# Query logits and key transposes in twos on two pairs of banks, and the inverse norms' product in the next step

## The chip, the cores and the metric

One core of a Trainium2 chip runs the whole program. The metric is device time in microseconds, the median over runs; smaller is better. PE is TensorE, DVE VectorE, ACT ScalarE, POOL GpSimd, SP the queue that issues most DMAs. Every engine takes its own instructions in order and waits at semaphores for the others.

## The reference

Cross attention with a channel softmax, then a gated feed-forward block on 4-bit weights, each added to a residual stream. Cut to what the kernel's stages compute:

```python
# x, ctx: (32, 64, 512).  Attention, 8 heads of 64:
q = Wq @ layernorm(x);  k = Wk @ ctx;  v = Wv @ ctx
q = softmax(q, over the head's 64 rows) * 64 ** -0.5
k = softmax(k, over the 512 columns)
context = einsum('bhdn,bhen->bhde', k, v)
out = einsum('bhde,bhdn->bhen', context, q)
out = Wo @ out + bo
out = out / max(norm(out, over rows), 1e-12) * g * 8
x = x + tanh(g_xattn) * out
# Feed-forward, inner width 1376, weights dequantised from 4 bits:
h = layernorm(x)
x = x + tanh(g_ffn) * ((silu(h @ Wg) * (h @ Wu)) @ Wd)
```

## The kernel before

The 32 batches go in 16 pairs of two times 64 rows, which fill 128 partitions. Attention runs as a software pipeline, one step for each pair `p` from 0 to 15, and a step `PAIRS` that drains it; the steps from 4 on are loops on the engines. The feed-forward block follows from about 402 us on. The change touches attention's steps from `p` = 2 on, called `residual` in the code; there are 14 of them.

In such a step PE works for three pairs at once. For pair `p` it computes query logits twice: transposed and rough in `t_logits` (for the maxima that DVE takes in `q_maxima`), and exact in `q_logits` with `less_max`, which subtracts the maxima. It computes key logits in `k_logits`, which DVE reduces in `k_maxima` and ACT exponentiates in `k_exps`, and transposes the exponentials in `k_transposed`. For pair `p - 1` it computes the query softmax's `denominators`, spreads their reciprocals over rows in `spread_reciprocals` (DVE multiplies with them in `normalise`), and builds `context` and `fold_context`. For pair `p - 2` it computes `output` and `squared_norms`, and `spread_inverse_norm` spreads the inverse norms over rows; DVE's `normed_and_gated` scales the output with them, and POOL adds it to the residual in `residual_added`.

The order of every engine's work is written out by hand, at the end of its `step` (PE L1293 to L1330, DVE L1685 to L1732, ACT L765 to L789, POOL L483 to L494). Four tiles t = 0 to 3 of 128 rows make up a pair's logits. PSUM's eight banks are four pairs: `dve_pair` for `t_logits` and the spread reciprocals; `k_pair` and `act_pair`, listed as `k_pairs`, on which `k_logits(t)` alternate; and `small_pair` for all sums of other kinds. In the part of a step after `q_max_rows`, `k_pair` holds the query logits of one tile after another (ACT's `q_exp_tile` reads them) and `act_pair` the key transposes of one tile after another (ACT's `k_transposed` reads them), so that PE waits on each for ACT's reading of the tile before.

The layernorm of the next pair runs in the same step: DVE's `layernorm_stats(p + 1)`, POOL's eight small instructions in `moments`, DVE's `layernorm_apply(p + 1)`, then ACT's `x_high(p + 1)`, which stands in ACT's order between the exponentials of key tiles 0 and 1. `k_logits(2)` and `k_logits(3)` wait until the exponentials of tiles 0 and 1 have been read out of their banks. The reciprocals of the denominators go through DMAs: ACT copies the sums out, SP reshapes them by four DMAs, DVE takes reciprocals, and SP gathers them by four more before `spread_reciprocals(0)`.

## Time and profile before

| what | us |
|---|---|
| median of 3 runs | 665.08 (663.89 to 665.49) |
| the profiled execution | 663.38 |
| its span, from the first to the last instruction | 661.5 |
| PE busy | 643.0 (97%) |
| DVE busy | 581.2 (88%) |
| ACT busy | 480.3 (73%) |
| POOL busy | 266.3 (40%) |

Busy shares are means over the whole span; what a wait costs has to be read from the stage in which it stands. PE's instructions overlap in the rows, since a matmul's modelled end lies after the next one's start: PE's own time is therefore read from start to start, and the difference between a row's start and the start of the next is what the row cost. The same holds, to a smaller degree, for DVE and ACT, whose next instruction may begin some 0.08 us ahead of the last one's end.

### The profile page before, as it was taken

Reading aid. Unit: us, or ns where it says so; the run is one execution under the profiler, and the core shown is the slowest. Engines: PE = TensorE matmul, PEld = TensorE weight load, DVE = VectorE, ACT = ScalarE, POOL = GpSimd, SP = SyncE. Lnnn points to the kernel's source line nnn. Section 1 sums busy time; section 2 is a strip of 40 time slices with the busy share of each in tenths; the row PEclk is TensorE's granted clock in tenths of the full one; section 3 lists DMA queues with packets and bytes.
Section 4 is the critical chain, followed back from the end, with each engine's and each line's share of the span. In section 5 each row is a group of like instructions: output and inputs, shape, how many; then the busy total and the mean of one; then the engine's idle time right before and its main releaser. Section 6 shows DMA issues by size and latency. Waiting matters only on the chain.

```text
span 661.5 us, 14311 instructions
## 1 busy us (share of the span) xinstructions
PE 643.0 (97%) x5097; PEld 330.9 (50%) x5097; DVE 581.2 (88%) x803; ACT 480.3 (73%) x846; POOL 266.3 (40%) x366
## 2 busy tenths in 40 slices
PE   7899999999999999999999998999999999999996
PEld 6454554555455456455445543445444544454443
DVE  7778898899899899889888849899999999988996
ACT  4886677677678667666767656778877887777775
POOL 6312323323332332332336265455444444444442
PEclk8999999999999999999999999999999999999999
DMA  4112422421340321222020000000000001000002
GB/s 120 37 34 76 100 53 56 103 78 27 102 95 15 94 82 40 50 82 78 12 86 21 6 10 2 1 1 0 1 33 32 1 1 44 22 0 17 37 12 63
DMA packets 30618, 28.57 MB, mean 43 GB/s; under 512 B 18623, under 2 KB 20810, under 8 KB 30578
## 3 DMA queue, kind: packets, MB, share of 16 engines
q1 hardware_dynamic: 28170, 27.37, 15.1%
q10 hardware_dynamic: 2408, 0.70, 0.5%
q8 instruction: 21, 0.34, 0.2%
q14 instruction: 19, 0.16, 0.1%
HBM read 22.06 MB, written 4.23 MB: 40 GB/s over the span
## 4 chain that ended last, share of the span: by engine, by line
PE 88%; ACT 4%; DVE 4%; issue 1%; POOL 1%; SPq 0%; DMA 0%; DVEq 0%; POOLq 0%
PE small_pair L1069 8%; PE pair L1358 8%; PE small_pair L1035 8%; PE pair L1359 7%; PE pair L1148 7%; PE pair L1021 6%; PE pair L1372 6%; PE pair L1381 6%; PE small_pair L1053 5%; PE pair L1178 4%; PE small_pair L1358 4%; PE pair L1133 4%; PE small_pair L1359 4%; ACT eq L682 3%; PE pair L1000 3%; PE pair L1158 2%
## 5 line engine op out<-in xcount | busy, mean ns | idle before, releaser
L1756 DVE SCALAR_TENSOR_TENSOR acc<-pair,scale_T,acc 128x512 f32<-128x512 f32 (+1 forms) x176 | 126.7, 747 | 12.1 <-PE pair L1359 5.9
L843 ACT ACTIVATE pair<-pair,rescale 128x512 f32<-128x512 f32 x119 | 74.9, 656 | 39.5 <-PE pair L1381 39.5
L1372 PE MATMUL pair<-in_hi,d_int 128*128 128x512 f32 (+1 forms) x176 | 100.7, 575 | 0.4 <-ACT in_hi L832 0.4
L1381 PE MATMUL pair<-in_lo,d_int 128*128 128x512 f32 (+1 forms) x176 | 100.2, 573 | 0.0
L673 ACT ACTIVATE ek<-pair,kneg 128x512 f32<-128x512 f32 x128 | 86.4, 682 | 17.9 <-DVE kneg L1617 17.9
L1358 PE MATMUL pair<-ek,w_gu 128*128 128x512 f16 (+1 forms) x235 | 91.1, 388 | 1.0 <-DVE acc L1756 0.7
L580 POOL TENSOR_TENSOR inter<-act_gate,acc 128x512 f32<-128x512 f32 (+1 forms) x43 | 55.0, 1278 | 86.7 <-ACT act_gate L825 86.7
L1359 PE MATMUL pair<-ekT,w_gu 128*128 128x512 f16 (+1 forms) x235 | 89.1, 379 | 0.0
L1622 DVE TENSOR_TENSOR eq<-eq,pair 128x1024 f32<-128x1024 f32 x64 | 77.7, 1213 | 11.0 <-PE pair L1133 11.0
L1612 DVE TENSOR_REDUCE qmax<-pair 128x16 f32<-128x1024 f32 x64 | 78.1, 1221 | 8.2 <-PE pair L1000 7.3
L682 ACT ACTIVATE eq<-pair 128x1024 f32<-128x1024 f32 x64 | 65.7, 1027 | 20.7 <-PE pair L1158 20.6
L1617 DVE TENSOR_REDUCE kneg<-pair 128x2 f32<-128x1024 f32 x64 | 77.8, 1216 | 0.5 <-PE pair L1021 0.3
L1756 DVE SCALAR_TENSOR_TENSOR acc<-small_pair,scale_T,acc 128x512 f32<-128x512 f32 (+1 forms) x88 | 65.8, 747 | 7.7 <-PE small_pair L1359 4.0
L589 POOL TENSOR_TENSOR in_lo<-inter,in_hi 128x512 fp32r<-128x512 f32 (+1 forms) x43 | 55.0, 1279 | 43.1 <-ACT in_hi L832 43.1
L678 ACT ACTIVATE ekT<-pair 128x1024 f32<-128x1024 f32 x64 | 65.4, 1022 | 5.3 <-PE pair L1178 5.3
L1069 PE MATMUL small_pair<-ekT,ctxT 128*64 128x512 f32 x256 | 64.6, 605 | 0.0
L461 POOL TENSOR_TENSOR rn_sq<-ss_max,minus_half 128x8 f32<-128x8 f32 x16 | 26.4, 1650 | 86.2 <-DVE ss_max L1546 86.2
L1035 PE MATMUL small_pair<-eq,fold 128*64 128x512 f32 x240 | 57.1, 598 | 0.0
L1178 PEld LDWEIGHTS pair<-ident,ek 64*128 64x128 f32 x1024 | 41.3, 138 | 21.5 <-issue 19.3
L1358 PEld LDWEIGHTS pair<-ek,w_gu 128*128 128x128 bf16 (+1 forms) x235 | 23.1, 98 | 54.7 <-issue 33.9
L1178 PE MATMUL pair<-ident,ek 64*128 64x64 f32 x1024 | 47.0, 226 | 0.8 <-ACT ek L673 0.7
L1358 PE MATMUL small_pair<-ek,w_gu 128*128 128x512 f16 (+1 forms) x117 | 45.4, 388 | 0.7 <-DVE acc L1756 0.7
(200 smaller groups left out, 1268.1 us busy)
## 6 DMA issues: line engine op xcount, KB each, us to landing
xall<-in_x SPq DMA_DIRECT2D x16, 256.0 KB, 2.6
ctx_raw<-in_ctx SPq DMA_DIRECT2D x16, 256.0 KB, 2.9
out_x<-xall SPq DMA_DIRECT2D x16, 256.0 KB, 2.0
zero<-zeros_plus SPq DMA_DIRECT2D x8, 344.0 KB, 5.9
packed<-in_L_ffn_gate_qweight SPq DMA_DIRECT2D x4, 688.0 KB
packed<-in_L_ffn_up_qweight SPq DMA_DIRECT2D x4, 688.0 KB
packed<-in_L_ffn_down_qweight SPq DMA_DIRECT2D x10, 256.0 KB
zero<-zeros_plus SPq DMA_DIRECT2D x5, 256.0 KB, 4.8
```

The lines of the kernel that those rows point to most:

```text
L673: act.activation(ek[:, b, t, :], k_pairs[t % 2][:, b, :], ACT.Exp, bias=kneg[:, b, t:t + 1], scale=-1.0, accum_out=ksum[:, k_slot(b, t):k_ ...
L682: act.activation(eq[:, par, t, :, :], k_pair[:, :, :], ACT.Exp).then_inc(q_exp, 1)
L1035: last = pe.matmul(small[1][half(b), :], fold[:, k_slot(b, t), :], eq[:, par, t, b, :], start=(t == 0), stop=(t == OT - 1))
L1069: last = pe.matmul(small[0][half(b), :].rearrange("c (t e d) -> c t e d", t=OT, e=2), ctxT[:, t, half(b)], heads, start=(t == 0), stop=(t ...
L1178: last = pe.transpose(act_pair[:, e, slot * DH:(slot + 1) * DH], ek[half(e), b, ot, t * P:(t + 1) * P], ident[half(e), half(e)])
L1358: pe.matmul(gu_bank[count % 3][0:w, :], lhsT, xT_hi[:, g, rows], start=True, stop=False)
L1359: pe.matmul(gu_bank[count % 3][0:w, :], lhsT, xT_lo[:, g, rows], start=False, stop=True).then_inc(gu_mm, 1)
L1372: pe.matmul(z_bank[nt], d_int[0:w, it, nt * P:(nt + 1) * P], in_hi[0:w, n % 2, :], start=it == 0, stop=False, skip_group_check=True)
L1381: pe.matmul(z_bank[nt], d_int[0:w, it, nt * P:(nt + 1) * P], in_lo[0:w, n % 2, :], start=False, stop=True, skip_group_check=True).then_inc ...
L1612: dve.tensor_reduce(qmax[:, t, :, 0:HEADS], dve_pair[:, :, :].rearrange("n b (h d) -> n b h d", d=DH), AX.X, ALU.max).then_inc(t_max, 1)
L1617: dve.tensor_reduce(kneg[:, :, t], k_pairs[t % 2][:, :, :], AX.X, ALU.min).then_inc(k_max, 1)
L1756: dve.scalar_tensor_tensor(out=acc[0:w, n % 2, m, :], in0=gu_bank[(8 * n + job) % 3][0:w, :], scalar=scale_T[0:w, it, 4 * m + g:4 * m + g ...
```

## The change

Three things change, all in steps from `p` = 2 on.

First, the banks and the order of the second part of a step. Query logits and key transposes of tile t both go to `k_pairs[t % 2]`. PE takes two tiles of query logits, then the two key transposes of the same tiles, then the next two of each; ACT reads them in the same order. A key transpose waits for ACT's exponentials of its own tile (same banks), query logits of tiles 2 and 3 wait for ACT's copies of the transposes of tiles 0 and 1, and the next step's `k_logits(0)` waits for the copy of transpose 2 in place of the last exponentials. `ctx_transposed` comes ahead of the transposes of tiles 2 and 3.

Second, `spread_inverse_norm` leaves the end of the step and stands in the next step between `k_logits(0)` and `denominators`, on bank `small[1]`; DVE's `normed_and_gated` follows to the next step, behind `k_maxima(0)`. `output(0)` then waits for it, and `denominators` no longer does.

Third, on DVE, `layernorm_stats` goes from ahead of `q_maxima(1)` to behind it, and `context_rows` from ahead of `normalise(3)` to behind it.

```diff
@@ -264,9 +264,7 @@
 
         def rn_bank(r2):
 
-            if not isinstance(r2, int):
-                return small[0][:, :]
-            return z_bank[0] if r2 == PAIRS - 2 else small[1 if r2 == PAIRS - 1 else 0][:, :]
+            return z_bank[0] if isinstance(r2, int) and r2 == PAIRS - 2 else small[1][:, :]
 
         def xT_bank(k):
 
@@ -275,6 +273,12 @@
         def y_rows():
 
             return small[1][:, :].bitcast(F16)[:, 0:N]
+
+        def q_pair(t, turns):
+            return k_pairs[t % 2 if turns else 0]
+
+        def kt_pair(t, turns):
+            return k_pairs[t % 2 if turns else 1]
 
         def y_columns(nt):
 
@@ -675,11 +679,11 @@
 
                 def k_transposed(t, back=0):
                     act.wait_ge(kt_mm, 4 * (p - back) + t + 1)
-                    act.activation(ekT[:, t, :, :], act_pair[:, :, :], ACT.Copy).then_inc(kt_evac, 1)
+                    act.activation(ekT[:, t, :, :], kt_pair(t, residual)[:, :, :], ACT.Copy).then_inc(kt_evac, 1)
 
                 def q_exp_tile(t):
                     act.wait_ge(q_mm, 4 * p + t + 1)
-                    act.activation(eq[:, par, t, :, :], k_pair[:, :, :], ACT.Exp).then_inc(q_exp, 1)
+                    act.activation(eq[:, par, t, :, :], q_pair(t, residual)[:, :, :], ACT.Exp).then_inc(q_exp, 1)
 
                 def denominators():
                     act.wait_ge(d_mm, r + 1)
@@ -784,6 +788,13 @@
                     context()
                     q_maxima()
                     k_exps(3)
+                if residual:
+                    for first_tile in (0, 2):
+                        q_exp_tile(first_tile)
+                        q_exp_tile(first_tile + 1)
+                        k_transposed(first_tile)
+                        k_transposed(first_tile + 1)
+                    return
                 for t in range(NT):
                     q_exp_tile(t)
                     k_transposed(t)
@@ -933,7 +944,9 @@
 
             def ffn_input(k):
 
-                if k == 3:
+                if k == 0:
+                    pe.wait_ge(kt_evac, 4 * PAIRS - 1)
+                elif k == 3:
                     pe.wait_ge(sT_ready, 4)
                 elif k == 2 * TPC:
                     pe.wait_ge(ss_evac, PAIRS)
@@ -1006,9 +1019,11 @@
                         return
                     if t == 0:
                         pe.wait_ge(c_lo, p + 1)
-                        if combine:
+                        if residual:
+                            pe.wait_ge(kt_evac, 4 * p - 1)
+                        if combine and isinstance(p, int) and p <= 2:
                             pe.wait_ge(q_exp, 4 * p)
-                        else:
+                        elif not combine:
                             pe.wait_ge(wT_lo_ready, 2)
                     elif t == 1:
                         if combine:
@@ -1041,10 +1056,7 @@
                     if not combine:
                         return
                     pe.wait_ge(q_exp, 4 * r + 4)
-                    if at_least(p, 3):
-                        pe.wait_ge(yn_ready, r - 1)
-                    else:
-                        pe.wait_ge(ct_evac, r + 1)
+                    pe.wait_ge(ct_evac, r + 1)
                     if isinstance(p, int) and p == 1:
                         pe.wait_ge(pool_consts, POOL_CONSTS)
                     for tt in range(2):
@@ -1140,12 +1152,16 @@
                     if t == 0:
                         pe.wait_ge(k_exp, 7 * p + 6)
                         pe.wait_ge(x_lo, p + 1)
+                    elif not residual:
+                        pe.wait_ge(q_exp, 4 * p + t)
+                    elif t == 1:
+                        pe.wait_ge(k_done, p + 1)
                     else:
-                        pe.wait_ge(q_exp, 4 * p + t)
+                        pe.wait_ge(kt_evac, 4 * p + t - 1)
                     cols = slice(t * P, (t + 1) * P)
                     for n, (w, v) in enumerate(((wqT_hi, xs_hi), (wqT_lo, xs_hi), (wqT_hi, xs_lo))):
                         for b in range(2):
-                            pe.matmul(k_pair[:, b, :], w[half(b), cols], v[half(b), par, :], start=(n == 0), stop=False)
+                            pe.matmul(q_pair(t, residual)[:, b, :], w[half(b), cols], v[half(b), par, :], start=(n == 0), stop=False)
 
                 def less_max(t):
                     if not project:
@@ -1155,7 +1171,7 @@
                         if not combine:
                             pe.wait_ge(wT_ready, 2)
                     for b in range(2):
-                        last = pe.matmul(k_pair[:, b, :], minus_spread[half(b), t, :], qmax_rows[half(b), :],
+                        last = pe.matmul(q_pair(t, residual)[:, b, :], minus_spread[half(b), t, :], qmax_rows[half(b), :],
                                          start=False, stop=True)
                     last.then_inc(q_mm, 1)
 
@@ -1163,7 +1179,9 @@
                     if not project:
                         return
                     pe.wait_ge(pool_consts, 2)
-                    if t > 0:
+                    if residual:
+                        pe.wait_ge(q_exp, 4 * p + t + 1)
+                    elif t > 0:
                         pe.wait_ge(kt_evac, 4 * (p - back) + t)
                     else:
                         pe.wait_ge(k_done, p + 1)
@@ -1175,7 +1193,7 @@
                             if residual:
                                 pe.wait_ge(ss_evac, r)
                         for e in range(2):
-                            last = pe.transpose(act_pair[:, e, slot * DH:(slot + 1) * DH],
+                            last = pe.transpose(kt_pair(t, residual)[:, e, slot * DH:(slot + 1) * DH],
                                                 ek[half(e), b, ot, t * P:(t + 1) * P], ident[half(e), half(e)])
                     last.then_inc(kt_mm, 1)
 
@@ -1195,15 +1213,16 @@
                     last.then_inc(ct_mm, 1)
 
                 def spread_inverse_norm():
-                    if not residual:
+                    if not at_least(p, 3):
                         return
-                    if isinstance(p, int) and p == 2:
+                    if isinstance(p, int) and p == 3:
                         pe.wait_ge(wT_ready, 3)
-                    pe.wait_ge(rn_gathered, 32 * r)
-                    pe.wait_ge(ct_evac, p + 1)
-                    pe.matmul(small[0][:, :], spread_batch[0:C, :], rn_rows[0:C, :], start=True, stop=True).then_inc(rn_mm, 1)
+                    pe.wait_ge(rn_gathered, 32 * (r - 1))
+                    pe.wait_ge(ct_evac, r + 1)
+                    pe.matmul(small[1][:, :], spread_batch[0:C, :], rn_rows[0:C, :], start=True, stop=True).then_inc(rn_mm, 1)
 
                 if drain:
+                    spread_inverse_norm()
                     denominators()
                     ffn_input(0)
                     ffn_input(1)
@@ -1292,6 +1311,7 @@
                     return
                 t_logits(0)
                 k_logits(0)
+                spread_inverse_norm()
                 denominators()
                 t_logits(1)
                 k_logits(1)
@@ -1312,21 +1332,20 @@
                 spread_reciprocals(0)
                 less_max(0)
                 context(3)
+                q_logits(1)
+                less_max(1)
                 k_transposed(0)
                 spread_reciprocals(1)
-                q_logits(1)
-                less_max(1)
                 k_transposed(1)
                 fold_context()
+                q_logits(2)
                 spread_reciprocals(2)
-                q_logits(2)
                 less_max(2)
-                k_transposed(2)
-                ctx_transposed()
-                spread_reciprocals(3)
                 q_logits(3)
                 less_max(3)
-                spread_inverse_norm()
+                spread_reciprocals(3)
+                ctx_transposed()
+                k_transposed(2)
                 k_transposed(3)
 
             step(0, 0, 0, True, False, False)
@@ -1685,9 +1704,11 @@
                 if project:
                     q_maxima(0)
                     k_maxima(0)
+                    if at_least(p, 3):
+                        normed_and_gated(p - 3)
+                    q_maxima(1)
                     if not last:
                         layernorm_stats(p + 1, i + par, 1 - par)
-                    q_maxima(1)
                     k_maxima(1)
                     if not last:
                         layernorm_apply(p + 1)
@@ -1699,6 +1720,7 @@
                     q_maxima(3)
                     k_maxima(3)
                 if drain:
+                    normed_and_gated(p - 3)
                     reciprocals()
                     second_stats(p - 3)
                     normalise(0)
@@ -1726,10 +1748,9 @@
                     less_zero(p, *weights, 1)
                 folded()
                 normalise(2)
+                normalise(3)
                 context_rows()
-                normalise(3)
                 key_sums()
-                normed_and_gated(r2)
 
             step(0, 0, 0, True, False, False)
             step(1, 0, 1, True, True, False)
```

## Rows read from the trace of the kernel before

**Rows 1.** The page, part 1: busy time, share of the span, instructions of each engine.

```profile
PE 643.0 (97%) x5097; PEld 330.9 (50%) x5097; DVE 581.2 (88%) x803; ACT 480.3 (73%) x846; POOL 266.3 (40%) x366
```

**Rows 2.** The windows view, one step: length, busy time of engines, granted clock, DMA.

```profile
181.40:205.20 23.80, 23.67 (x245) 12.41 (x242) 21.79 (x28) 17.11 (x31) 7.77 (x14) 1.00 0.30 71
```

**Rows 3.** The timeline of PE in one step: start, duration, line, operation, count.

```profile
184.35 0.71 PE L1178 MATMUL pair<-ident,ek 64*128 64x64 f32 x16
184.87 0.47 PE L1133 MATMUL pair<-rden_rows,spread 64*128 64x512 f32 x2
...
185.87 0.41 PE L1158 MATMUL pair<-qmax_rows,minus_spread 64*128 64x512 f32 x2
186.28 0.71 PE L1178 MATMUL pair<-ident,ek 64*128 64x64 f32 x16
...
187.55 0.50 PE L1133 MATMUL pair<-rden_rows,spread 64*128 64x512 f32 x2
...
188.80 0.66 PE L1178 MATMUL pair<-ident,ek 64*128 64x64 f32 x16
...
189.71 0.50 PE L1133 MATMUL pair<-rden_rows,spread 64*128 64x512 f32 x2
...
191.11 0.39 PE L1204 MATMUL small_pair<-rn_rows,spread_batch 64*128 64x512 f32 x1
...
191.80 0.50 PE L1000 MATMUL pair<-wqT_hi,xs_hi 64*128 64x512 f32 x2
192.40 0.50 PE L1021 MATMUL pair<-cs_hi,wkT_hi 64*128 64x512 f32 x2
...
193.29 1.92 PE L1053 MATMUL small_pair<-eq,head_sum 128*32 128x512 f32 x16
195.15 0.50 PE L1000 MATMUL pair<-wqT_hi,xs_hi 64*128 64x512 f32 x2
...
201.77 0.40 PE L1021 MATMUL pair<-cs_hi,wkT_hi 64*128 64x512 f32 x2
...
205.20 0.46 PE L1094 MATMUL pair<-ident,qmax 64*128 64x64 f32 x8
```

**Rows 4.** The timeline of PE, seven steps later.

```profile
359.60 1.92 PE L1053 MATMUL small_pair<-eq,head_sum 128*32 128x512 f32 x16
```

**Rows 5.** The timeline of DVE; in brackets the idle time before and what ended it.

```profile
188.45 1.21 DVE L1622 TENSOR_TENSOR eq<-eq,pair 128x1024 f32<-128x1024 f32 x1
...
191.60 0.70 DVE L1553 SCALAR_TENSOR_TENSOR yn<-small_pair,gate_col,y 128x512 f32<-128x512 f32 x1
192.34 1.23 DVE L1612 TENSOR_REDUCE qmax<-pair 128x16 f32<-128x1024 f32 x1
...
194.61 0.68 DVE L1455 BATCH_NORM_STATS2 stats<-xall 128x6 f32 x1
195.69 1.22 DVE L1612 TENSOR_REDUCE qmax<-pair 128x16 f32<-128x1024 f32 x1 [0.40 <-PE pair L1000]
...
200.10 0.55 DVE L1626 RECIPROCAL rden<-den_sq 128x64 f32<-128x64 f32 x1 [1.00 <-DMA den_sq<-den]
...
201.26 1.23 DVE L1612 TENSOR_REDUCE qmax<-pair 128x16 f32<-128x1024 f32 x1
```

**Rows 6.** The timeline of ACT in the same step.

```profile
186.32 1.03 ACT L682 ACTIVATE eq<-pair 128x1024 f32<-128x1024 f32 x1 [0.19 <-PE pair L1158]
...
191.32 1.02 ACT L682 ACTIVATE eq<-pair 128x1024 f32<-128x1024 f32 x1 [0.37 <-PE pair L1158]
...
198.53 0.63 ACT L642 ACTIVATE xs_hi<-xn 128x512 fp32r<-128x512 f32 x1 [1.31 <-DVE xn L1461]
...
200.30 0.20 ACT L673 ACTIVATION_READ_ACCUMULATOR ek<-pair,kneg 128x1 f32 x1
```

**Rows 7.** The timeline of POOL: the first and the last of layernorm's eight instructions.

```profile
195.37 0.19 POOL L86 TENSOR_TENSOR ln_work<-stats 128x2 f32<-128x2 f32 x1 [1.57 <-DVE stats L1455]
...
197.26 0.55 POOL L86 TENSOR_TENSOR ln_work<-ln_work,minus_half 128x1 f32<-128x1 f32 x1
```

## Prediction

> **What bounds the kernel now.** I read the page's busy shares first: PE 97%, DVE 88%, ACT 73% [rows 1]. Then the windows view of one step of attention, to see whether that holds where the change is: in 23.8 us PE is busy 23.67, DVE 21.79, ACT 17.11, and the granted clock is 1.00, the level of 2.4 GHz [rows 2]. So PE comes first, but DVE has only 2 us to spare. Then the timelines, from start to start. The product `denominators` starts at 193.29 and, seven steps later, at 359.60 [rows 3, 4]: 166.31 / 7 = 23.76 us a step, and what is said of one step holds for all of them, 14 with the edits.
>
> I count from PE's `t_logits(0)` at 191.80. `k_logits(0)` starts at +0.60, `denominators` +1.49, `t_logits(1)` +3.35, `k_logits(3)` +9.97, `q_max_rows` +13.40; from `q_max_rows` to the next `t_logits(0)` is 23.76 - 13.40 = 10.36 [rows 3]. The reader is to see two things. PE's waits are short: `k_logits(0)` starts 0.06 after ACT's last query exponential (191.32 + 1.02), some 0.3 late [rows 3, 6]; the key transposes of tile 1 start at 186.28, 0.2 after `less_max(1)` from 185.87 would have let them [rows 3]. Together with smaller ones, at `spread_reciprocals` and `t_logits(3)`, I make it about 1.2 us a step. And between +2.8 and +8.7 a chain runs over three engines: DVE's `layernorm_stats` (194.61, 0.68 long), POOL's eight instructions (195.37 to 197.81), DVE's `layernorm_apply`, ACT's `x_high` (198.53), then the exponentials of key tile 1, whose last record ends at 200.50 [rows 5, 6, 7]. `k_logits(3)`, which needs their banks, starts at 201.77 [rows 3]: 1.27 us of slack. DVE waits 1.00 us for the denominators' DMA before its reciprocals at 200.10 [rows 5].
>
> **The change part by part.**
>
> *First half of a step, to `q_max_rows`.* `k_logits(0)` now waits for ACT's copy of transpose 2 (below), and starts at about +0.78 in place of +0.60. The norm's product comes behind it. At the end of the step it costs 0.2 now (the transposes beside it take 191.11 to 191.80, 0.69; those of tile 0 took 184.35 to 184.87, 0.52) [rows 3]; in front of `denominators` I give it 0.23, one pair of products: five pairs took 187.55 to 188.80, 1.25, and four 184.87 to 185.87, 1.00 [rows 3], so about 0.23 a pair and 0.1 ahead of the first, where the shape of the tiles changes. So `denominators` starts at 0.78 + 0.89 + 0.23 = +1.9 (0.89 is 192.40 to 193.29), and `t_logits(1)` 1.86 later (193.29 to 195.15), at +3.75, 0.4 late [rows 3].
>
> On DVE `normed_and_gated` (191.60 to 192.34, 0.74) goes from ahead of `q_maxima(0)` to behind `k_maxima(0)` [rows 5]. The end of a step gains nothing by it: `t_logits(0)` doesn't ask for it. It ends at +3.6, ahead of `output(0)` at about +4.9, which now waits for it with all later PE work behind; that wait costs nothing. POOL's addition behind it fits before layernorm's instructions.
>
> But `q_maxima(1)` can't start before `t_logits(1)` + 0.54 (195.69 - 195.15), +4.29 [rows 3, 5], and `layernorm_stats` now stands behind it: it starts at 4.29 + 1.14 = +5.43 in place of +2.81. (1.14 is 192.34 on to the next start in the same engine, 1.23 long less the 0.08 by which instructions overlap.) The chain follows: stats end +6.11; POOL's instructions take 197.81 - 195.29 = 2.52 from that end [rows 5, 7], +8.63; `layernorm_apply` then ends at about +9.2 and `x_high` starts at +9.25 in place of +6.73. From `x_high` to the end of tile 1's exponentials is 200.50 - 198.53 = 1.97 [rows 6], so +11.22, and `k_logits(3)` starts at +11.27. PE would be there at 9.97 + 0.4 = +10.35: a new wait of 0.9, with all of PE's later work queued behind it. On ACT `k_exps(1)`, `outputs` and `k_exps(2)` queue behind `x_high`.
>
> DVE is held too: it reaches `layernorm_apply` at +7.2 and waits there 1.5 for POOL. The 1.00 before the reciprocals is eaten by this. Behind `layernorm_apply` stands `second_stats`, as long as the first statistics' 0.68, so the reciprocals start at about +9.75 in place of +8.30, so `q_maxima(2)` 1.16 later (200.10 to 201.26) at +10.90 [rows 5], `q_maxima(3)` two reductions later at +13.17, ending +14.4; `squared_norms` asks for that end, and `q_max_rows` follows at +14.8 (now 205.20, 0.43 behind 201.26 + 2.28 + 1.23 [rows 3, 5]). Both paths give the same: **+1.4 us** in the first half. Their gathering DMAs start as much later and land before `spread_reciprocals(0)` still.
>
> *Second half, 10.36 now.* Up to the end of `context(3)` nothing changes: 184.35 - (205.20 - 23.76) = 2.91 [rows 3]. Then `q_logits(1)` and `less_max(1)`: four pairs, 0.91, and 0.1 for the change of shape: to 3.93. Transposes of tile 0: 0.52, to 4.45; spread 0.32 (a pair and a change), to 4.77. The transposes of tile 1 now need ACT's exponentials of tile 1. Their `less_max` ends at 4.09, ACT starts 0.04 later and takes 1.03 (186.28 to 186.32, then 1.03 [rows 3, 6]), the transposes follow 0.14 after its end: 5.31. A wait of 0.54 where 0.2 stood. Transposes and fold 1.27 (186.28 to 187.55): 6.58. `q_logits(2)` 0.79, spread 0.23, `less_max` 0.23, `q_logits(3)` 0.68, `less_max` 0.23: 8.74. The spread of tile 3 waits for `normalise(2)`: the spread of tile 2 starts at 7.37, DVE at 7.81, and 1.21 later [rows 5] it is 9.02, so 9.08, a wait of 0.34. Then spread 0.33, `ctx_transposed` and transposes 2 together 0.91 (188.80 to 189.71 [rows 3]), transposes 3 0.52: 10.84, and `normalise(3)` ends just there, so the next `t_logits(0)` is at 10.88. **+0.5 us.** Transposes 2 end at about 10.55, ACT's copy 1.03 later: `k_logits(0)` at +0.78 after `t_logits(0)`, counted above.
>
> What the new order removes: query logits no longer wait for the exponentials just before them. Of tile 2 that wait was nil, as the five pairs at 0.23 and a change show. The loads of the pair after next are issued behind `ctx_transposed`, later in the step; they have the rest of a step, so nothing. `context_rows` behind `normalise(3)` ends before the norm's product wants it, except in the drain, which has no logits to cover it: 0.3.
>
> *The sum.* A full step gains 1.4 + 0.5 = 1.9 to 2.0 us. Twelve steps (3 to 14): 23.6. Step 2 has no inverse norm yet but the late statistics: 1.5. Step 15 has no layernorm: its first half loses only 0.4, so with the second half and the drain's wait 1.3. Together **26.4 us**. The profiled execution took 663.38, so 689.8; it lies 1.7 under the median of the runs, 665.08, and the same difference put on that gives **691 us**.
>
> What no row shows is how PE restarts after its new waits. After a wait the first product of a query tile takes about 0.1 more, since its weights weren't loaded ahead. With none of it the step gains 1.7, with twice it 2.3: 24 to 31 in all.
>
> The Trainium skill (Perfetto Trace Analysis, Matmuls) says that independent matmul groups should rotate through different PSUM banks, so that evacuation of one overlaps the matmuls of the next. That rule speaks for this change. The rows agree with it, but show that little is left to win: 187.55 to 188.80 runs without a wait although each kind of tile keeps to its own pair.
>
> **The rivals.**
>
> *Faster: PE becomes the only bound.* If ACT's reading of two tiles hides behind PE's work on the other two, the 1.2 us of waits go, and the chain behind the statistics is hidden as well. PE's own work is 23.76 - 1.2, about 22.55 a step: 14 x 1.2 = 17 us less, 648. It decides if tile 1's exponentials are read before `k_logits(3)` wants them, at +10.3. For it speaks the 1.27 of slack; against it that the statistics move by 2.6, twice as much. The rule of the Trainium skill named above would make it come out so.
>
> *A smaller loss: the late layernorm is hidden*, in POOL or by an earlier `q_maxima(1)`, and only the order of the second half and the norm's product cost: 0.9 a step, 13 in all, 678. For it speaks that step 15 must look so. Against it: DVE takes its work in order, and nothing else releases `q_maxima(1)`.
>
> *The change doesn't do what it says*: new waits just replace the old ones, within 0.3%, 663 to 667. Against it stand both halves of the sum.
>
> *Worse*: the waits of the two halves add to longer ones, over 700. A lower granted clock would do it as well. Against it: the new waits are each under 1 us by the sum, and the step read has 1.00 [rows 2]; no row shows the level of 1.2 GHz in attention.
>
> **How the numbers follow.** About 0.3%, 2 us, is what a measurement of this kernel can tell from no change. Forecast (683 to 699): 0.76. Smaller loss (670 to 683): 0.12. Faster: 0.05. No change: 0.03. Worse: 0.04. Range 678 to 699: the forecast, and the nearer half of the smaller loss. Faster by over 0.3% 0.05, same 0.03, slower 0.92.
>
> **What would show it.** In the profile after, steps of 25.6 to 25.9 us. PE idle before `k_logits(3)`, ended by ACT's exponentials, 0.9. DVE idle before `layernorm_apply`, ended by POOL, 1.5, and no longer any before the reciprocals. PE idle before the transposes of tile 1, ended by ACT's query exponentials, 0.5, and before the spread of tile 3, ended by DVE. `q_max_rows` +14.8 after `t_logits(0)`, `t_logits(0)` +10.9 after that. It is wrong if `x_high` starts before +8, or if `k_logits(3)` doesn't wait.

## The result, and the profile after

The changed kernel takes 696.61 us (695.7 to 697.47), the kernel before beside it 664.87 (663.89 to 665.49): a ratio of 1.0479, 95% interval 1.0458 to 1.05. The profiled execution took 697.22 us, its span is 694.6. It is slower, in the forecast's own range (683 to 699, point 691), and 5.6 us past the point.

From here on a step is counted from PE's `denominators` to the next, which start at 182.42 and 208.57 in the step shown. The twelve full steps (3 to 14) take 313.74 us together, 26.14 each, where [rows 3, 4] gave 23.76: 28.6 us. Step 2 takes 25.35 (23.86 before), step 15 takes 23.92 (22.93): 1.5 and 1.0. These 31.1 are the change. The profiled execution is 33.8 longer than the one before, 663.38; 1.9 of the rest lie ahead of the first changed step, whose `denominators` start at 52.51 in place of 50.63. Nothing in the program differs there, and in the kernels below they start at 50.5 to 52.7. The granted clock is at 0.50 for 10.24 us of that stretch, and for 3.41 us in the execution before; how much of the 1.9 comes from it is not shown. The other 0.8 lie behind the last step and outside the span.

The page's busy line and the windows view of one step (length, then busy time of PE, PEld, DVE, ACT, POOL, granted clock, DMA share, GB/s) answer [rows 1, 2]:

```profile
PE 650.2 (94%) x5097; PEld 331.1 (48%) x5097; DVE 592.2 (85%) x803; ACT 478.7 (69%) x846; POOL 271.6 (39%) x366
...
180.85:206.90 26.05, 24.07 (x242) 12.33 (x243) 22.62 (x28) 16.90 (x32) 8.18 (x14) 1.00 0.26 65
```

PE was busy for all but 0.1 us of a step and now lacks 2.0; the granted clock is still 1.00, the level of 2.4 GHz, and stays there from 25.2 us to 690.8. DVE has the same 803 instructions, yet 11 us more busy time. That is the first sign of something that the prediction did not have: a wait that the profile counts as work.

The timeline of PE in that step answers [rows 3] (in brackets: idle time before, and what ended it):

```profile
180.85 0.49 PE L1013 MATMUL pair<-wqT_hi,xs_hi 64*128 64x512 f32 x2
181.30 0.50 PE L1036 MATMUL pair<-cs_hi,wkT_hi 64*128 64x512 f32 x2
...
182.11 0.38 PE L1222 MATMUL small_pair<-rn_rows,spread_batch 64*128 64x512 f32 x1
182.42 1.92 PE L1065 MATMUL small_pair<-eq,head_sum 128*32 128x512 f32 x16
184.28 0.50 PE L1013 MATMUL pair<-wqT_hi,xs_hi 64*128 64x512 f32 x2
...
191.79 0.50 PE L1036 MATMUL pair<-cs_hi,wkT_hi 64*128 64x512 f32 x2 [0.75 <-ACT ek L677]
...
193.32 0.49 PE L1013 MATMUL pair<-wqT_hi,xs_hi 64*128 64x512 f32 x2 [0.56 <-DVE qmax L1631]
...
195.97 0.46 PE L1106 MATMUL pair<-ident,qmax 64*128 64x64 f32 x8
...
201.29 0.72 PE L1196 MATMUL pair<-ident,ek 64*128 64x64 f32 x16 [0.42 <-ACT eq L686]
...
205.08 0.50 PE L1145 MATMUL pair<-rden_rows,spread 64*128 64x512 f32 x2 [0.16 <-DVE eq L1641]
...
206.90 0.51 PE L1013 MATMUL pair<-wqT_hi,xs_hi 64*128 64x512 f32 x2
```

The bracketed waits are where PE's idle time stands: `k_logits(3)` on ACT's key exponentials, `t_logits(3)` on DVE's maxima, the key transposes of tile 1 on ACT's query exponentials, the spread of tile 3 on DVE. From `t_logits(0)` to `q_max_rows` is 15.12 us, and 10.93 from there to the next `t_logits(0)`; the prediction said 14.8 and 10.88.

The timelines of DVE, ACT and POOL between those points answer [rows 5 to 7]:

```profile
183.65 0.74 DVE L1572 SCALAR_TENSOR_TENSOR yn<-small_pair,gate_col,y 128x512 f32<-128x512 f32 x1
184.82 1.23 DVE L1631 TENSOR_REDUCE qmax<-pair 128x16 f32<-128x1024 f32 x1 [0.42 <-PE pair L1013]
185.96 0.68 DVE L1474 BATCH_NORM_STATS2 stats<-xall 128x6 f32 x1
...
189.19 0.55 DVE L1480 TENSOR_SCALAR xn<-xall,ln_work 128x512 f32 x1 [1.42 <-POOL ln_work L86]
...
190.25 0.54 DVE L1645 RECIPROCAL rden<-den_sq 128x64 f32<-128x64 f32 x1
190.82 1.05 DVE L1649 CAST rden_parts<-rden 128x64 fp32r<-128x64 f32 x1
191.91 0.22 DVE L1651 TENSOR_TENSOR rden_parts<-rden,rden_parts 128x64 fp32r<-128x64 f32 x1
192.05 1.22 DVE L1631 TENSOR_REDUCE qmax<-pair 128x16 f32<-128x1024 f32 x1
...
189.77 0.63 ACT L646 ACTIVATE xs_hi<-xn 128x512 fp32r<-128x512 f32 x1 [3.42 <-DVE xn L1480]
...
190.54 1.28 POOL L480 TENSOR_TENSOR xs_lo<-xn,xs_hi 128x512 fp32r<-128x512 f32 x1 [1.39 <-ACT xs_hi L646]
```

The chain of the late statistics is there as forecast: statistics behind `q_maxima(1)`, DVE idle for 1.42 ahead of `layernorm_apply`, `x_high` 8.92 after `t_logits(0)`. But look at the cast at 190.82. It moves 128x64 numbers, and takes 1.05 us. Its end, 191.87, is 0.05 after the end of POOL's `x_low` (190.54 + 1.28 = 191.82). In the trace before, the same two instructions are

```profile
199.30 1.27 POOL L476 TENSOR_TENSOR xs_lo<-xn,xs_hi 128x512 fp32r<-128x512 f32 x1 [1.50 <-ACT xs_hi L642]
...
200.78 0.19 DVE L1630 CAST rden_parts<-rden 128x64 fp32r<-128x64 f32 x1
```

with the cast 0.21 behind `x_low`'s end, and 0.19 long. In the changed kernel all twelve casts of steps 3 to 14 overlap `x_low` and take 0.95 to 1.05; the others take 0.2, but for step 1's.

### The profile page after: what moved, and what is told of

It is laid out like the page before. It is cut to its first block, busy times and chain, and to the rows that moved or that the text cites. A ratio compares the mean times of both kernels' runs of the same rounds, so it can differ in the third digit from the quotient of the medians.

```text
span 694.6 us, 14312 instructions
## 1 busy us (share of the span) xinstructions
PE 650.2 (94%) x5097; PEld 331.1 (48%) x5097; DVE 592.2 (85%) x803; ACT 478.7 (69%) x846; POOL 271.6 (39%) x366
## 4 chain that ended last, share of the span: by engine, by line
PE 62%; DVE 18%; issue 8%; POOL 6%; ACT 4%; POOLq 0%; DVEq 0%; SPq 0%; DMA 0%
PE pair L1377 8%; PE pair L1378 7%; PE small_pair L1081 6%; PE pair L1164 6%; PE pair L1391 6%; PE pair L1400 6%; DVE qmax L1631 4%; DVE eq L1641 4%; PE small_pair L1377 4%; POOL ln_work L86 4%; PE small_pair L1378 4%; ACT eq L686 3%; PE pair L1145 3%; DVE rden_parts L1649 2%; POOL xall L485 2%
## 5 line engine op out<-in xcount | busy, mean ns | idle before, releaser
L686 ACT ACTIVATE eq<-pair 128x1024 f32<-128x1024 f32 x64 | 64.3, 1027 | 28.9 <-PE pair L1174 28.9
L682 ACT ACTIVATE ekT<-pair 128x1024 f32<-128x1024 f32 x64 | 63.7, 1023 | 6.1 <-PE pair L1196 6.1
L485 POOL TENSOR_TENSOR xall<-xall,yn 128x512 f32 (+1 forms) x16 | 20.5, 1284 | 96.5 <-DVE yn L1572 96.5
L1196 PE MATMUL pair<-ident,ek 64*128 64x64 f32 x1024 | 41.7, 225 | 6.4 <-ACT eq L686 5.9
```

Source lines behind the costliest of these rows:

```text
L686: act.activation(eq[:, par, t, :, :], q_pair(t, residual)[:, :, :], ACT.Exp).then_inc(q_exp, 1)
```

## The experiments

The theory after the comparison: in the first half, two separate things cost. The late statistics make ACT's exponentials late for `k_logits(3)` (forecast), and `x_low` holds DVE's cast (called the collision from here on), so that `q_maxima(2)` and all behind it come some 0.8 us later (not forecast). The second half's order costs 0.6. The rival: there is one loss, the late layernorm, and the long cast is only a way in which DVE spends time that it would have waited.

**POOL's order swapped.** The changed kernel, and `ctx_low` ahead of `x_low`.

```diff
-                    x_low(p + 1, 1 - par)
                     ctx_low(p + 1, 1 - par)
+                    x_low(p + 1, 1 - par)
```

> The changed kernel with one edit on POOL: the low part of the context is made before the low part of x, so that POOL's x_low no longer runs while DVE casts the reciprocals. If that cast (1.05 us in the changed kernel, 0.19 before) waits for POOL, it is back at 0.2 and a step goes from 26.14 to about 25.4 us: 687 to 689 in all. If the long cast only stands where DVE would have waited anyway, the step stays within 0.1 and the time at 696.

Measured: 686.16 us (685.36 to 686.87), ratio 1.0326 (1.0309 to 1.0343); steps 25.3 to 25.4; a little under the 687 to 689 expected. DVE and POOL:

```profile
185.83 0.20 DVE L1649 CAST rden_parts<-rden 128x64 fp32r<-128x64 f32 x1
...
188.56 1.27 POOL L475 TENSOR_TENSOR cs_lo<-ctx_raw,cs_hi 128x512 fp32r<-128x512 f32 x1 [4.40 <-ACT cs_hi L642]
189.79 1.28 POOL L480 TENSOR_TENSOR xs_lo<-xn,xs_hi 128x512 fp32r<-128x512 f32 x1
```

With `x_low` elsewhere every cast of steps 3 to 14 is 0.20 again, and 10.5 us are back. The statistics are as late as in the changed kernel, so the collision is a term of its own: 0.8 us a step.

**Statistics ahead.** The changed kernel, and `layernorm_stats` ahead of `q_maxima(1)`, as before.

```diff
-                    q_maxima(1)
                     if not last:
                         layernorm_stats(p + 1, i + par, 1 - par)
+                    q_maxima(1)
```

> The changed kernel with layernorm_stats back ahead of q_maxima(1). If the late statistics are the largest term, x_high comes about 1.1 us earlier, k_logits(3) no longer waits, and a step falls by 1.0 to 1.2 to about 25.0: 682 to 685. The cast still meets x_low, since both move together. If the order of the second half is the largest term, the step falls by less than 0.5: 691 or more.

Measured: 684.2 us (683.22 to 684.91), ratio 1.029 (1.0273 to 1.0307); steps 25.1 to 25.4. PE no longer waits before `k_logits(3)`; 12.4 us are back. But the collision stays:

```profile
183.39 0.55 DVE L1480 TENSOR_SCALAR xn<-xall,ln_work 128x512 f32 x1 [1.10 <-POOL ln_work L86]
...
185.25 0.84 DVE L1649 CAST rden_parts<-rden 128x64 fp32r<-128x64 f32 x1
...
184.75 1.30 POOL L480 TENSOR_TENSOR xs_lo<-xn,xs_hi 128x512 fp32r<-128x512 f32 x1 [1.39 <-ACT xs_hi L646]
```

DVE still waits for POOL ahead of `layernorm_apply`, because `normed_and_gated`, now ahead of the statistics, delays them by itself. So the reciprocals follow `layernorm_apply` with a wait of at most 0.25 for their DMA, where it was 0.81 to 1.11 before, and the cast meets `x_low`.

**Banks and second half undone.** The changed kernel with query logits on one pair and key transposes on the other, and the second half's order on PE, ACT and DVE as before; the norm's product and the late statistics stay. The core of it, on PE:

```diff
-                q_logits(1)
-                less_max(1)
                 k_transposed(0)
                 spread_reciprocals(1)
+                q_logits(1)
+                less_max(1)
                 k_transposed(1)
```

> The changed kernel with banks and order of the second half as before; the inverse norms' product stays in the next step and the statistics stay late. By the sum the second half goes from 10.9 back to 10.3 us and the rest stays: step about 25.5, 688 to 690. If the pairs of banks were the largest term, the step falls below 24.8: under 680.

Measured: 688.09 us (687.84 to 688.29), ratio 1.035 (1.0333 to 1.0367); steps 25.63. The second half is 10.33 again, the first half 15.3. So the new banks with their order cost 8.5 us, 0.6 a step in the second half (forecast: 0.5), and give back some 0.15 in the first.

**The late statistics alone.** The kernel before, and only `layernorm_stats` behind `q_maxima(1)`.

```diff
-                    if not last:
-                        layernorm_stats(p + 1, i + par, 1 - par)
                     q_maxima(1)
+                    if not last:
+                        layernorm_stats(p + 1, i + par, 1 - par)
```

> The kernel before with one edit: layernorm_stats behind q_maxima(1). By the chain x_high starts 1.1 to 1.8 us later, k_logits(3) waits, and the cast may meet x_low: step 24.7 without that meeting, 25.3 with it, 677 to 685 in all. If only the whole change together makes the chain late, the step stays at 23.8 and the time at 665.

Measured: 684.39 us (684.21 to 684.52), ratio 1.0295 (1.0278 to 1.0313); steps 25.41, casts 0.95 to 1.05. One line of the change alone makes nearly 20 of the 31 us, 1.65 a step, with the collision in it. On PE:

```profile
186.46 0.50 PE L1021 MATMUL pair<-cs_hi,wkT_hi 64*128 64x512 f32 x2 [0.74 <-ACT ek L673]
187.99 0.50 PE L1000 MATMUL pair<-wqT_hi,xs_hi 64*128 64x512 f32 x2 [0.56 <-DVE qmax L1612]
```

The same two waits as in the changed kernel, to 0.01.

**The norm's move alone.** The changed kernel with banks and second half undone as above and the statistics ahead: only `spread_inverse_norm` in the next step and `normed_and_gated` behind `k_maxima(0)` are left.

```diff
                     k_maxima(0)
+                    if at_least(p, 3):
+                        normed_and_gated(p - 3)
                     if not last:
                         layernorm_stats(p + 1, i + par, 1 - par)
                     q_maxima(1)
...
-                normed_and_gated(r2)
```

> Of the change only the inverse norm's product in the next step and normed_and_gated behind k_maxima(0) stay; banks, the order of the second half and layernorm_stats are as before. If the move of the norm costs only its place on PE (some 0.1 to 0.2 us a step ahead of denominators), 666 to 668. If DVE's 0.75 us between k_maxima(0) and layernorm_stats also pushes POOL's x_low onto the cast of the reciprocals, as in the run with the statistics early (casts 0.84 to 1.07 there), 674 to 677, with casts near 1.0 in steps 3 to 14. That run minus the one with late statistics alone would have the norm at 3.7 us (688.09 - 684.39).

Measured: 674.9 us (674.19 to 675.6), ratio 1.0158 (1.0141 to 1.0175); steps 24.6. DVE and POOL:

```profile
180.81 0.55 DVE L1465 TENSOR_SCALAR xn<-xall,ln_work 128x512 f32 x1 [0.98 <-POOL ln_work L86]
...
182.47 1.03 DVE L1634 CAST rden_parts<-rden 128x64 fp32r<-128x64 f32 x1
...
182.16 1.29 POOL L480 TENSOR_TENSOR xs_lo<-xn,xs_hi 128x512 fp32r<-128x512 f32 x1 [1.39 <-ACT xs_hi L646]
```

By itself the move costs 0.85 a step, nearly all of it in the first half (14.3 in place of 13.4), and the casts are long. The parts don't add: norm and late statistics alone cost 11.0 and 19.7 over the kernel before beside them, together (688.09) 23.4. That fits a collision that either of them brings about and that both together pay once: 7.3 drop out.

**Both remedies.** Statistics ahead and POOL's order swapped, on the changed kernel.

```diff
-                    q_maxima(1)
                     if not last:
                         layernorm_stats(p + 1, i + par, 1 - par)
+                    q_maxima(1)
...
-                    x_low(p + 1, 1 - par)
                     ctx_low(p + 1, 1 - par)
+                    x_low(p + 1, 1 - par)
```

> The changed kernel with both single remedies at once: layernorm_stats ahead of q_maxima(1), and ctx_low ahead of x_low on POOL. If the late statistics and the collision of x_low with the cast are two separate terms, their gains add: 696.6 - 12.4 - 10.4 = 674 (672 to 677), casts 0.20. If both remedies relieve the same stretch of DVE ahead of q_maxima(2), the second adds little: 682 to 685.

Measured: 676.31 us (675.07 to 678.37), ratio 1.0177 (1.0155 to 1.0198). The gains add: 20.3 of the expected 22.8, and most steps take 24.5. The rival of one loss has fallen. Steps 4 to 7, though, take 24.9 to 25.6: in steps 5 to 7 DVE waits 0.40 to 1.04 for the reciprocals' DMA again, and in step 4 PE waits 0.45 for the gathering of the reciprocals. That stays open until the next runs.

**The fold ahead.** As the last; on PE the second half is reordered, and the waits that the fold needs stand at the last transposes of tile 0:

```diff
                 spread_reciprocals(1)
-                k_transposed(1)
                 fold_context()
-                q_logits(2)
+                k_transposed(1)
                 spread_reciprocals(2)
+                q_logits(2)
```

> As the run with both remedies, and on PE the fold goes ahead of the key transposes of tile 1 and the spread of tile 2 ahead of the query logits of tile 2. If the second half's wait before the transposes of tile 1 is a term of its own that other PE work can cover, 0.3 to 0.5 us a step less than that run: 668 to 671 beside 674 to 675. If the end of the step is set by DVE's normalise all the same, no difference to that run.

Measured: 669.02 us (668.66 to 669.43), ratio 1.0073 (1.0056 to 1.009). The fold fills PE's wait for ACT ahead of the transposes of tile 1. That wait is gone, and so is the one ahead of the spread of tile 3: the undisturbed steps go from 24.5 to 23.9.

**The norm first.** As the last (pairs of banks, statistics ahead, POOL swapped, fold ahead), but DVE takes `normed_and_gated` directly behind `q_maxima(0)`, and on PE the spread of tile 1 and the transposes of tile 2 come one place earlier.

```diff
                     q_maxima(0)
-                    k_maxima(0)
                     if at_least(p, 3):
                         normed_and_gated(p - 3)
+                    k_maxima(0)
                     if not last:
                         layernorm_stats(p + 1, i + par, 1 - par)
...
+                spread_reciprocals(1)
                 k_transposed(0)
-                spread_reciprocals(1)
...
                 spread_reciprocals(3)
-                ctx_transposed()
                 k_transposed(2)
+                ctx_transposed()
                 k_transposed(3)
```

> Banks in twos as in the changed kernel, but normed_and_gated directly behind q_maxima(0), layernorm_stats behind k_maxima(0) (ahead of q_maxima(1)), ctx_low ahead of x_low, and PE's second half as: query logits 1, spread 1, key transposes 0, fold, key transposes 1, spread 2, query logits 2 and 3, spread 3, key transposes 2, context transposes, key transposes 3. If all losses of the change come from the order of the work and not from the banks, a step takes 23.1 to 23.5 us, 656 to 661. If the pairs of banks themselves cost (PE restarting after waits), 667 to 672.

Measured: 665.29 us (663.94 to 667.06), ratio 1.001 (0.9994 to 1.0026): no difference to the kernel before, and between the two forecasts. Steps 10 to 14 take 23.5, which is less than before's 23.76, so the pairs of banks need not cost anything. But steps 3 to 9 take 23.8 to 24.9. SP and DVE in one of them, whose `denominators` start at 221.27:

```profile
219.69 0.43 SPq L335 DMA_DIRECT2D ctx_raw<-in_ctx  x1
220.16 0.43 SPq L365 DMA_DIRECT2D zero<-zeros_plus  x1
220.64 0.64 SPq L370 DMA_DIRECT2D packed<-in_L_ffn_up_qweight  x1
223.89 2.77 SPq L318 DMA_DIRECT2D den_sq<-den  x4
230.18 2.67 SPq L323 DMA_DIRECT2D rden_rows<-rden_parts  x4
...
229.11 0.56 DVE L1645 RECIPROCAL rden<-den_sq 128x64 f32<-128x64 f32 x1 [1.33 <-DMA den_sq<-den]
```

The reciprocals start 7.84 after the denominators there, 7.3 to 8.4 in steps 3 to 9, and 6.9 in steps 10 to 14. The small transfers of the denominators (8 KB each) are issued 2.6 us after the last of 1.5 MB of loads, 2.1 to 2.8 in steps 3 to 9; in the trace before the gap was 4.2 us in the same step, and 3.0 to 4.3 in steps 3 to 9:

```profile
214.87 0.64 SPq L366 DMA_DIRECT2D packed<-in_L_ffn_up_qweight  x1
...
219.68 2.77 SPq L314 DMA_DIRECT2D den_sq<-den  x4
```

**Zeros first.** As the last, and SP issues the load of the weights' zeros ahead of its wait for the context transposes.

```diff
+                if following and residual:
+                    load_zeros(p + 1, *following)
                 if project and more:
                     sp.wait_ge(ct_mm, p + 1)
                     load(p + 2, par)
```

> The run with the norm first and nothing but this: SP issues the load of the weights' zeros (344 KB) ahead of the wait for the context transposes and of the pair's loads, in place of behind them. In the run with the norm first, the bulk loads of steps 3 to 9 are issued only 2.4 us ahead of the denominators' small transfers and those steps take 23.8 to 24.9 in place of 23.5, reciprocals 7.3 to 8.4 us behind the denominators in place of 6.9. If the small transfers queue behind the bulk, the reciprocals come back to about 7.0 to 7.4 in those steps and 665.3 falls to 660 to 662. If those steps are slow for another reason, no change, 664 to 666.

Measured: 663.2 us (660.2 to 665.01), ratio 0.9975 (0.9959 to 0.9991). The time lies between the two forecasts; the reciprocals decide. They are back at 6.7 to 7.1 in all steps but one (7.5), and the steps at 23.5 to 23.6 but for two of 23.8 and 24.0. The DMA packets of the traces say the same: in steps 3 to 9 the last packet of the loads ends 3.8 to 5.0 us after the first small transfer is issued with the norm first, 1.5 to 2.9 with the zeros first, and 2.0 to 3.2 in the kernel before. So the small transfers did wait for the bulk. What is left is the other side of it: in the step of 24.0 DVE waits 1.07 for the pair's rows ahead of `layernorm_stats`.

**All weights first.** The packed words, too, go ahead of the pair's loads.

```diff
+                if following and residual:
+                    load_weights(p + 1, *following)
                 if project and more:
                     sp.wait_ge(ct_mm, p + 1)
                     load(p + 2, par)
```

> As the last, but all of the weights' loads (zeros and packed words, 1.03 MB in steps 3 to 9) go ahead of the pair's loads. If the small transfers queue behind the bulk, the same start of the bulk gives the same 660 to 662, unless the pair's x then lands too late for layernorm_stats, which shows as DVE idle ahead of it, 0.3 to 1.5 us a step in those steps: 661 to 668. If the queue isn't the reason, 664 to 666.

Measured: 699.37 us (698.35 to 699.93), ratio 1.052 (1.05 to 1.054); steps up to 29.6. This missed even the upper bound. DVE:

```profile
218.87 0.70 DVE L1476 BATCH_NORM_STATS2 stats<-xall 128x6 f32 x1 [3.07 <-DMA ctx_raw<-in_ctx]
```

The mechanism named is there, the pair's rows landing late, but twice as late as thought (2.9 to 3.8 in steps 3 to 9); 1 MB of weights stand ahead of them, and the whole chain of layernorm with it. That is not all of the loss. The windows view of steps 3 and 4, with the granted clock third from the end:

```profile
74.11:100.58 26.47, 23.46 (x242) 12.23 (x242) 21.76 (x28) 17.11 (x31) 7.76 (x14) 1.00 0.29 66
100.58:130.19 29.61, 26.31 (x242) 13.10 (x242) 21.80 (x28) 17.11 (x31) 7.73 (x14) 0.88 0.26 65
```

DVE waits 3.59 for the rows in the first and 3.81 in the second, and PE then stands idle for 2.8 ahead of `k_logits(3)` in both. But the second is 3.1 longer: within PE's idle time, from 111.71 on, the granted clock is 0.50, the level of 1.2 GHz, for 6.83 us. In steps 4 to 9 it is there for 27.3 us together, and in the full steps of no other run. Why it did not fall in step 3 is not shown.

**Context transposes earlier.** As with the zeros first, and on PE:

```diff
+                ctx_transposed()
                 spread_reciprocals(3)
                 k_transposed(2)
-                ctx_transposed()
                 k_transposed(3)
```

> The run with the zeros first, and on PE the context transposes go ahead of the spread of tile 3 (behind less_max of tile 3), so that the pair's loads are issued some 0.9 us earlier. If the queue behind the bulk is what still costs in steps 3 to 9, 0.3 to 0.9 us less in each of them, against 0.2 us more in every step for normalise(3) starting later: 657 to 661. If not, 2 to 3 us more than that run.

Measured: 667.41 us (664.82 to 676.73), ratio 1.0071 (1.0044 to 1.0099). The trace is of the fastest execution, 664.82. Its quiet steps take 23.6, 0.1 more (said 0.2); but steps of 24.6, 25.2 and 24.1 remain, the worst with DVE waiting 2.05 for the pair's rows. Issuing the loads earlier didn't remove the late landings, and the time is 4.2 over the run with the zeros first, beyond both forecasts: the expectation failed. Why the rows land later here was not settled.

**The pair's x early.** As with the zeros first; x of the next pair has a slot of its own and needs no wait, so SP issues it directly behind the norms' gather.

```diff
+                if residual and project and more:
+                    sp.dma_start(xall[:, p + 2, :], x_rows[p + 2]).then_inc(loaded[par], 16)
                 if residual:
                     sp.wait_ge(rn_ready, 2 * r2 + 2)
```

> As the run with the zeros first, and SP issues the load of the next pair's x directly behind the norms' gather (it writes a slot of its own, so that it needs no wait for the context transposes); the context's load stays behind the transposes. If the spread of the run with the zeros first (steps of 23.5 to 24.0, 660.2 to 665.0) comes from the bulk loads at the end of a step landing late, for layernorm_stats or for the reciprocals, all steps from 2 on come to 23.5, 659 to 661.5. If another cause makes them vary, 662 to 664 as that run.

Measured: 661.05 us (660.31 to 662.05), ratio 0.9946 (0.9932 to 0.9959): 0.5% faster than the kernel before. All steps from 2 to 14 take 23.5 but one (23.96, DVE waiting 0.86 for the pair's rows). By the packets the loads' last one ends only 1.1 to 1.9 us after the first small transfer is issued in steps 3 to 9, and before it in steps 10 to 14:

```profile
206.36 0.46 SPq L394 DMA_DIRECT2D xall<-in_x  x1
211.58 1.18 SPq L398 DMA_DIRECT2D rn_rows<-rn_parts  x2
212.80 0.47 SPq L363 DMA_DIRECT2D zero<-zeros_plus  x1
214.24 0.33 SPq L405 DMA_DIRECT2D ctx_raw<-in_ctx  x1
214.61 0.64 SPq L374 DMA_DIRECT2D packed<-in_L_ffn_up_qweight  x1
218.88 0.71 SPq L318 DMA_DIRECT2D den_sq<-den  x1
```

Whether the kernel before would gain the same by SP's order alone, or with its own banks, was not tried.

## Why the prediction was right, and where its terms were off

**The late statistics** were right in kind and nearly in size. Measured from `t_logits(0)`: `t_logits(1)` +3.43 (said +3.75), statistics +5.11 (+5.43), `x_high` +8.92 (+9.25), `k_logits(3)` +10.94 (+11.27) after a wait of 0.75 (0.9), DVE idle 1.42 (1.5). All are 0.3 earlier, by one term: `k_logits(0)` came at +0.45 to +0.55, not +0.78. ACT's copy of transpose 2 ended earlier than the sum had it. The spread of tile 3 starts where it was put (+9.11 after `q_max_rows`, said +9.08), but the context transposes and the transposes of tile 2 behind it took 0.75 together, not the 0.91 of [rows 3]. The late statistics alone then cost 1.65 a step in their own run, with the collision in it.

**`q_maxima(2)`** is the term that failed. The prediction put it 1.16 behind the reciprocals, from [rows 5]; it was 1.80 (190.25 to 192.05). The reciprocals were 0.35 early (+9.40, said +9.75), `q_maxima(2)` 0.3 late (+11.20, said +10.90), and so was `q_max_rows` (+15.12, said +14.8). The duration of the cast was taken from a row in which POOL had just finished. The 1.00 us in which DVE waits for its DMA [rows 5] was not merely slack that the new wait "eats": it was what kept the cast behind `x_low`. Without it the cast would have started at 199.78, in the middle of `x_low` (199.30 to 200.57). The trace of before had one instance of the collision, in step 1:

```profile
34.52 1.29 POOL L476 TENSOR_TENSOR xs_lo<-xn,xs_hi 128x512 fp32r<-128x512 f32 x1 [4.60 <-ACT xs_hi L642]
...
35.22 0.64 DVE L1630 CAST rden_parts<-rden 128x64 fp32r<-128x64 f32 x1
```

The cast's end, 35.86, is 0.05 after `x_low`'s 35.81, as in the changed kernel. Of 16 casts of before only this one is longer than 0.2. Whoever looks at the longest record of each instruction, not only at its usual one, can find the missing term before the change is built. By the prediction's own times `x_low` runs from about +10.0 (0.77 behind `x_high`) to +11.3, and the cast starts at +10.4 (0.68 behind the reciprocals); held until `x_low` ends it takes an estimated 0.9, 0.7 more than its 0.2, which is most of the 0.8 a step that the swap on POOL gave back.

**The norm's product** costs PE the 0.23 that was said: from `k_logits(0)` to `denominators` it is 1.12 (181.30 to 182.42), before 0.89 (192.40 to 193.29). Its larger price was on DVE: `normed_and_gated` ahead of the statistics delays layernorm enough for the collision, 0.85 a step alone. The prediction followed DVE there only as far as `output(0)`.

**The second half** was said to gain 0.5 to 10.88; it is 10.92 to 11.03. The waits stand where forecast, 0.42 and 0.16 (said 0.54 and 0.34). The 0.1 that was put on the first product behind a wait shows at `k_logits(3)`: 0.34 (191.79 to 192.13), where its next ones take 0.23. Undoing this part alone gave back 0.5 a step in all.

**Ends.** Step 2 has the forecast 1.5. Step 15 came to 1.0 with the drain's wait in it, said 1.3 together. The errors partly cancel: 0.3 too much for `k_logits(0)`, 0.64 too little behind the reciprocals. A full step costs 2.38 more, just above the largest that the prediction had allowed for (2.3), and the 31.1 in all are at the top of its 24 to 31. That the time lies inside the range owes something to a range that was drawn wider than that.

**The loads** moved behind `ctx_transposed` were costed at nothing, since "they have the rest of a step". In the changed kernel that holds: the reciprocals come 7.83 behind the denominators in every full step, set by DVE, and no DMA is waited for. It is a cost hidden under a larger one. Once the first half was mended it appeared, up to 1.4 us a step, and the last four runs are about nothing else.

**The rivals.** "Faster" fell where the prediction said it would: tile 1's exponentials came after `k_logits(3)` wanted them. The rule of the Trainium skill that stood beside it (Perfetto Trace Analysis, Matmuls: independent groups rotate through banks) did not pay by itself here: the banks with their order cost 8.5 us. With another order around them a step takes 23.5 in place of 23.76. What the same order would give on the old banks was not tried, so no run shows a gain from the rotation. "A smaller loss" needed the layernorm hidden: with both remedies 676.31, beside 678 forecast for it, though part of that is the late small transfers in steps 4 to 7; its undisturbed steps lose 0.7, said 0.9. "Worse" asked for longer waits or a lower granted clock: the clock stayed at 1.00.

## What to carry to other kernels

Before an instruction is moved, look for what its old place kept apart: list, for each short instruction on the path, its longest record besides its usual one, and ask what the other engine was doing. A wait that looks like slack may be what keeps two engines off each other. Of a step that is moved later, follow the DMAs that hang on it into the next step as well, to the small transfers that queue behind them; they cost nothing only as long as something else is later.

## What the runs showed of the hardware

A DVE cast of 128x64 takes 0.2 us alone. Started while POOL's 128x512 subtraction runs, it ends 0.05 us after POOL does, whenever it started: 0.95 to 1.05 in the twelve full steps of the changed kernel, 0.48 to 1.07 over all runs, and busy in the profile all the time. The reciprocals are not held: in the kernel before 14 of 16 start while `x_low` runs, as the one at 200.10 does [rows 5], and all of them take 0.55. DVE's unpacking of the weights (`nibbles`, 128x1376) is: with POOL's order swapped `x_low` runs beside it, and it takes 0.98 to 1.08 in steps 3 to 9 in place of 0.93. The Trainium skill (SBUF — State Buffer, Who interferes with whom) says that DVE's copies and casts can take a port pair that they share with GpSimd, that whoever issues first holds it for the whole instruction, and that the other is blocked, not slowed. The trace agrees in the cast's end.

Small transfers on SP's queue wait for the bulk issued ahead of them: with the last of 1.5 MB issued 2.1 to 2.8 us earlier the reciprocals started 7.3 to 8.4 us behind the denominators, and mostly 6.8 when 344 KB of it had gone some 6.0 us ahead of them in place of 3.3 to 3.8. The Trainium skill (DMA: Bandwidth & Descriptors, Queues, rings and completion order) says that on each DMA engine descriptors are consumed in the order of the ring. The runs here agree with that; they don't tell waiting in order from a sharing of the engines' time.
